# Expert layers of a routed language-model block: per-expert results summed in PSUM instead of stored and reloaded, and both layers of a group taken in a row

## The reference, cut to what matters

```python
# b = 32 sequences, s = 128 tokens, d = 256; E = 32 experts, K = 8, hidden width 1024
probs = jax.nn.softmax(x @ gate_w.T + gate_b, axis=-2)
vals, idx = top_k(probs, K, over the tokens)           # per sequence and expert
merged = jnp.einsum('bked,bke->bed', tok, vals)        # tok: the picked rows of x
h = gelu(jnp.einsum('bei,eih->beh', concat(merged, 1), w1))   # w1: 32 x 257 x 1024
o = jnp.einsum('bej,ejo->beo', concat(h, 1), w2)              # w2: 32 x 1025 x 256
out_tok = jnp.einsum('beo,bke->bkeo', o, vals)
out = zeros.at[b, idx].add(out_tok)                    # each pick's weighted result to its token
return h2 + out
```

## Time and profile before

| | us |
|---|---|
| median of 3 runs | 860.63 (858.05 to 862.29) |
| profiled execution, whole | 859.29 |
| its span, first to last instruction | 857.5 |
| PE, DVE, ACT, POOL busy in the span | 704.5, 608.4, 348.6, 447.3 |

### The profile page before, as it was taken

The page is one execution under the profiler, slowest core; times in us unless marked ns, Lnnn a source line. Parts: engine busy times, 40 slices in busy tenths (PEclk is TensorE's granted clock), DMA queues, the critical chain, the costliest instruction groups (busy, mean ns, idle before and its releaser), DMA issues. The chain is left out here.

```text
span 857.5 us, 20594 instructions
## 1 busy us (share of the span) xinstructions
PE 704.5 (82%) x7892; PEld 484.9 (57%) x7892; DVE 608.4 (71%) x863; ACT 348.6 (41%) x553; POOL 447.3 (52%) x250
## 2 busy tenths in 40 slices
PE   6577679878999999999999999994899859866755
PEld 4356544437777777777777777763677624322333
DVE  3688558889999999999999999992477631001124
ACT  3366534443544545544554444542455431100000
POOL 1788300004999999999999999992121100000000
PEclk9699989997999999999999999996999969999998
DMA  4100000000001010000000000002953159999985
GB/s 113 50 2 0 0 0 0 0 1 15 14 14 34 14 37 12 12 6 12 12 12 11 8 12 12 15 15 61 412 180 121 49 225 387 415 420 417 416 274 196
DMA packets 47295, 85.89 MB, mean 100 GB/s; under 512 B 5552, under 2 KB 30192, under 8 KB 47120
## 3 DMA queue, kind: packets, MB, share of 16 engines
q1 hardware_dynamic: 41920, 81.07, 25.8%
q10 hardware_dynamic: 5328, 4.17, 1.6%
HBM read 76.04 MB, written 9.18 MB: 99 GB/s over the span
## 5 line engine op out<-in xcount | busy, mean ns | idle before, releaser
L909 POOL TENSOR_TENSOR read<-state,q_pos 128x1024 f32<-128x1024 f32 x128 | 300.3, 2365 | 28.7 <-DVE state L1018 22.5
L1018 DVE TENSOR_TENSOR_SCAN state<-fac,ps_up 128x1024 f32<-128x1024 f32 x128 | 290.0, 2277 | 8.6 <-ACT fac L953 8.2
L953 ACT ACTIVATE fac<-ps_xf 128x1016 f32<-128x1016 f32 x128 | 130.3, 1018 | 175.7 <-PE ps_xf L1052 162.4
L1052 PEld LDWEIGHTS ps_xf<-hot,xtab 64*128 64x128 f32 x2048 | 126.6, 190 | 58.0 <-ACT fac L953 43.8
L1052 PE MATMUL ps_xf<-hot,xtab 64*128 64x128 f32 x2048 | 149.5, 286 | 10.9 <-ACT fac L953 8.8
L1052 PE MATMUL ps_up<-hot,utab 64*128 64x128 f32 x2048 | 140.8, 277 | 17.5 <-DVE state L1018 17.5
L1052 PEld LDWEIGHTS ps_up<-hot,utab 64*128 64x128 f32 x2048 | 127.2, 190 | 23.0 <-issue 16.4
L918 POOL TENSOR_TENSOR utab<-tab 128x1024 f32 (+1 forms) x32 | 64.5, 2016 | 94.6 <-SPq L86 94.6
L1097 PE MATMUL ps_o<-read,misc 128*32 128x256 f32 x1024 | 82.1, 392 | 4.1 <-POOL read L909 4.1
L1008 DVE TENSOR_TENSOR xtab<-tab,ps_k 128x1024 f32<-128x1024 f32 x64 | 59.5, 929 | 2.0 <-PE ps_k L1044 2.0
L1692 DVE COPY h_t<-ps_e 128x512 f32<-128x512 f32 x16 | 10.3, 686 | 59.6 <-PE ps_e L1756 59.6
(11 more groups left out here) (233 smaller groups left out, 973.7 us busy)
## 6 DMA issues: line engine op xcount, KB each, us to landing
early<-in_L_ffn_w SPq DMA_DIRECT2D x19, 2048.0 KB, 17.7
pair_tab<-in_L_ffn_w SPq DMA_DIRECT2D x5, 2048.0 KB, 23.4
late<-in_L_ffn_w SPq DMA_DIRECT2D x3, 2048.0 KB, 23.5
zy<-in_L_ffn_w SPq DMA_DIRECT2D x3, 1536.0 KB, 21.8
rec_out<-osb SPq DMA_DIRECT2D x128, 32.0 KB, 1.5
late<-rec_out SPq DMA_DIRECT2D x8, 512.0 KB, 4.1
pair_tab<-in_L_ffn_w SPq DMA_DIRECT2D x4, 512.0 KB, 3.5
early<-in_L_ffn_w SPq DMA_DIRECT2D x2, 1024.0 KB, 24.6
```

What stands on the lines that cost most here:

```text
L909: nc.gpsimd.tensor_tensor(read[n % 2][:], state[n % 4][:].rearrange("p (b i t) -> p b i t", b=2, i=IB), q_pos[x.s][:, :, x.k].unsqueeze(2) ...
L953: nc.scalar.activation(fac[n % 2][:].rearrange("p (n t) -> p n t", t=T)[:, :, 1:], ps_x[:].rearrange("p (n t) -> p n t", t=T)[:, :, 1:], A ...
L1018: nc.vector.tensor_tensor_scan(state[n % 4][:], fac[n % 2][:], ps_u[n % 2][:], 0.0, ALU.mult, ALU.add)\
L1052: last = nc.tensor.matmul(dst[:, b * 512 + col * T:b * 512 + (col + 1) * T], stationary[rows], pos[rows], start=True, stop=True)
```

## The change

All eight groups take the same way. The order of the blocks is first layer and second layer of group 0, then of group 1, and so on. `ps_1` is there once, in the PSUM banks in which the transposes also land; the four banks that it leaves hold `ps_s`, the results in their final arrangement, over the whole part. After the first layer of group g, PE runs `spread_rows(g-1)`: eight products of a zero-one matrix, cut out of a wide tile `spread` at a shifted column, with `eo`, which add the group g-1 into all rows of `ps_s`. So `exp_out`, its six stores, its four reloading transfers, the zeroing of `oq` and the sum on DVE are gone; DVE copies `ps_s` to `oq` once (L1684 of the changed kernel). Group 7 keeps its own way. `eo` is there once. The biases of both layers lie in one tile `bias`, and `sel` therefore is written on 64 partitions by two copies in place of one. The last block is one transfer like all others. The helpers `strip` and the reordered zero-one matrix `by_row` are made in the freed slot after group 5.

```diff
@@ def expert_halves():
-    order = [(1, g, h) for g in range(2) for h in range(2)]
-    for g in range(X // QB):
-        order += [(2, g, h) for h in range(2)]
-        if g + 2 < X // QB:
-            order += [(1, g + 2, h) for h in range(2)]
-    return order
+    return [(layer, g, h) for g in range(X // QB) for layer in (1, 2) for h in range(2)]
@@ def experts(nc, a, m, sem, sb, out):
-    eo = sb("eo", [P, 2, E])
+    eo = sb("eo", [P, E])
+    spread = sb("spread", [P, QUADS * P + X])
...
-        ps_1 = [ps[:, 2 * s:2 * s + 2].rearrange("p n c -> p (n c)") for s in range(2)]
+        ps_s = ps[:, 0:4].rearrange("p n (q e) -> p (n q) e", e=E)
+        ps_1 = ps[:, 4:6].rearrange("p n c -> p (n c)")
         ps_t = ps[:, 4:6].rearrange("p n (h q) -> p (n h) q", q=P)
@@ scalar
-            def store(g):
-                act.wait_ge(eo_ok, START + g + 1)
-                act.dma_start(exp_out[QB * g:QB * (g + 1)].rearrange("x b e -> (x b) e"),
-                              eo[:, g % 2]).then_inc(eo_st[g % 2], 16)
-
             for g in range(GROUPS):
                 hidden(g)
-                if 0 < g < GROUPS - 1:
-                    store(g - 1)
                 if g + 2 < GROUPS:
                     selections(g + 2)
-            act.wait_ge(row_ok, ZEROS)
-            src = exp_out.rearrange("x (q j) e -> j x q e", j=QB)
-            for j in range(QB):
-                act.dma_start(oq[j * X:j * X + STORED], src[j, 0:STORED]).then_inc(f_ld, 16)
@@ sync
-                if n < len(wt.order) - 1:
-                    wt.load_all(sp, n)
-                else:
-                    wt.transfer(sp, n, 0, QB, slice(0, HID // 2)).then_inc(wt_head, 16)
-                    wt.load(sp, n, 0, QB, slice(HID // 2, HID))
+                wt.load_all(sp, n)
@@ vector
             for g in range(GROUPS):
...
                 if g == GROUPS - 1:
-                    dve.wait_ge(row_mm, SPREAD_MM)
-                    dve.wait_ge(f_ld, START + 16 * QB)
-                    nc.vector.tensor_tensor(oq, oq, ps_s, ALU.add).then_inc(row_ok, 1)
+                    dve.wait_ge(sp_mm, START + GROUPS - 1)
+                    nc.vector.tensor_copy(oq, ps_s).then_inc(row_ok, 1)
                 results(g)
+                if g == GROUPS - 3:
+                    ch.link(nc.vector.memset(strip, 0.0))
+                    nc.vector.tensor_copy(by_row, ident[:].rearrange("p (n j) -> p j n", j=QB))
+                    nc.vector.tensor_copy(strip.rearrange("p (x q) -> p q x", q=QUADS)[:, QUADS - 1, 0:QB],
+                                          at_row[:, X - QB:X]).then_inc(row_ok, 1)
+                    dve.wait_ge(pick_mm, START + 1)
+                    nc.vector.tensor_copy(last_picks, ps_t).then_inc(row_ok, 1)
@@ tensor
             def first_layer(g):
-                s = g % 2
-                pe.wait_ge(gl, START + g - 1)
+                if g > 0:
+                    pe.wait_ge(htok, START + 2 * g)
...
+            def spread_rows(g):
+
+                pe.wait_ge(row_ok, SPREAD)
+                pe.wait_ge(eo_ok, START + g + 1)
+                for q in range(QUADS):
+                    at = q * P + X - QB * (g + 1)
+                    last = nc.tensor.matmul(ps_s[:, q], spread[:, at:at + P], eo[:], start=g == 0 and q % 2 == 0, stop=g == GROUPS - 2,
+                                            skip_group_check=True)
+                last.then_inc(sp_mm, 1)
...
-            first_layer(0)
-            first_layer(1)
-            for g in range(GROUPS - 1):
+            for g in range(GROUPS):
+                first_layer(g)
+                if g > 0:
+                    spread_rows(g - 1)
                 transpose_hidden(g)
-                second_bias(g)
-                for h in range(2):
-                    second_layer(g, h)
+                second_layer(g)
                 if g == GROUPS - 3:
                     picks_of_last()
-                if g + 2 < GROUPS:
-                    first_layer(g + 2)
-                if g == GROUPS - 3:
-                    pe.wait_ge(row_ok, PICKS)
-
-            transpose_hidden(GROUPS - 1)
-            second_bias(GROUPS - 1)
-            spread_rows()
-            second_layer(GROUPS - 1, 0)
+
             pe.wait_ge(row_ok, SUMS)
             output_stored(0)
-            second_layer(GROUPS - 1, 1)
             rows_of_last()
```

More of the change, by code:

```diff
@@ L32 @@
 HT = HID // P
-STORED = X - 2 * QB
 EPS = 1e-5
@@ L1582, in experts @@
 def experts(nc, a, m, sem, sb, out):
-    ident, merged, exp_out, h2, picked = m["ident"], m["merged"], m["exp_out"], m["h2"], m["picked"]
-    wt, stored = m["wt"], m["stored"]
-    b1, b2 = sb("b1_sb", [X, HID]), sb("b2_sb", [X, E])
-    sel = [sb(f"sel{s}", [X, QB, B]) for s in range(2)]
+    ident, merged, h2, picked = m["ident"], m["merged"], m["h2"], m["picked"]
+    wt, late = m["wt"], m["stored"]
+    bias = sb("bias", [2 * X, HID])
+    b1, b2 = bias[0:X], bias[X:2 * X, 0:E]
+    sel = [sb(f"sel{s}", [2 * X, QB, B]) for s in range(2)]
     hg = sb("hg", [P, HID])
     h_t = sb("h_t", [P, HT, P])
-    eo = sb("eo", [P, 2, E])
-    oq = stored[:, 0:QUADS * E].rearrange("p (q e) -> p q e", e=E)
-    last_picks = stored[:, QUADS * E:QUADS * (E + T)].rearrange("p (q t) -> p q t", t=T)
-    last_rows = stored[:, QUADS * (E + T):QUADS * (E + T) + E]
-    strip = sb("strip", [P, QUADS + X])
+    eo = sb("eo", [P, E])
     at_row, at_expert = sb("at_row", [P, B]), sb("at_expert", [P, X])
-    spread = merged[:, 0]
+    spread = sb("spread", [P, QUADS * P + X])
+    oq = late[:, 0:QUADS * E].rearrange("p (q e) -> p q e", e=E)
+    last_picks = late[:, QUADS * E:QUADS * (E + T)].rearrange("p (q t) -> p q t", t=T)
+    last_rows, by_row, strip = (late[:, lo:lo + n] for lo, n in ((3072, E), (3328, P), (3456, QUADS + X)))
     GROUPS = X // QB
@@ L1631, in selections @@
                     after(act, 2, g - 2, 1)
-                nc.scalar.copy(sel[g % 2][:], ident[0:X, QB * g:QB * (g + 1)].unsqueeze(2)
-                               .broadcast_to([X, QB, B])).then_inc(sel_ok, 1)
+                for lo in (0, X):
+                    last = nc.scalar.copy(sel[g % 2][lo:lo + X], ident[lo:lo + X, lo + QB * g:lo + QB * (g + 1)]
+                                          .unsqueeze(2).broadcast_to([X, QB, B]))
+                last.then_inc(sel_ok, 1)
             def hidden(g):
@@ L1757, in transpose_hidden, with second_layer @@
                     last.then_inc(ht, 1)
-            def second_bias(g):
-                pe.wait_ge(eo_ok, START + g - 1)
-                nc.tensor.matmul(ps_2[g % 2][:, 0:E], sel[g % 2][:].rearrange("x j b -> x (j b)"), b2[:],
+            def second_layer(g):
+                if g > 1:
+                    pe.wait_ge(eo_ok, START + g - 1)
+                nc.tensor.matmul(ps_2[:, g % 2], sel[g % 2][X:2 * X].rearrange("x j b -> x (j b)"), b2,
                                  start=True, stop=False, skip_group_check=True)
-            def second_layer(g, h):
-                s = g % 2
-                n_half = wt.at[2, g, h]
-                if n_half == len(wt.order) - 1:
-                    pe.wait_ge(wt_head, START + 16)
-                else:
-                    wt.wait(pe, n_half)
-                pe.wait_ge(htok, START + 2 * g + h + 1)
-                for n in range(h * HT // 2, (h + 1) * HT // 2):
-                    if n_half == len(wt.order) - 1 and n == HT - HT // 4:
+                for n in range(HT):
+                    h, at = divmod(n, HT // 2)
+                    n_half = wt.at[2, g, h]
+                    if at == 0:
@@ L1774, in second_layer @@
                         wt.wait(pe, n_half)
+                        pe.wait_ge(htok, START + 2 * g + h + 1)
                     for j in range(QB):
-                        last = nc.tensor.matmul(ps_2[s][j * B:(j + 1) * B, 0:E], h_t[:, n, j * B:(j + 1) * B],
-                                                wt.block(n_half, j, slice(n % (HT // 2) * E, (n % (HT // 2) + 1) * E)),
+                        last = nc.tensor.matmul(ps_2[j * B:(j + 1) * B, g % 2], h_t[:, n, j * B:(j + 1) * B],
+                                                wt.block(n_half, j, slice(at * E, (at + 1) * E)),
@@ L1789, in picks_of_last @@
                                                 start=True, stop=True)
-                last.then_inc(row_mm, 1)
-            def spread_rows():
-                pe.wait_ge(row_ok, SPREAD)
-                pe.wait_ge(gl, START + GROUPS)
-                for q in range(QUADS):
-                    last = nc.tensor.matmul(ps_s[:, q], spread[:, QB * q:QB * (q + 1)].rearrange("p j x -> p (j x)"),
-                                            eo[:, 0], start=True, stop=True)
-                last.then_inc(row_mm, 1)
+                last.then_inc(pick_mm, 1)
+                pe.wait_ge(row_ok, PICKS)
             def rows_of_last():
```

71 lines of the change are left out of this document (29 added, 42 removed).

## The result

| | before | changed |
|---|---|---|
| median, us | 859.34 (857.78 to 862.29, 4 runs) | 848.42 (845.83 to 850.42, 4 runs) |
| profiled execution, whole | 859.29 | 850.42 |
| its span | 857.5 | 848.7 |
| PE's first product of the experts' part | 703.20 | 701.42 |
| copy of the last `eo` | 839.81 | 830.64 |

The ratio of the changed kernel to the one before is 0.9869, with a 95% interval of 0.9843 to 0.9894: 1.3% faster, clear of the noise, and the median lies 1.2 us from the 849.6 that was forecast.

The account below looks back on a forecast made before the run. Weight transfers set the pace, then the reload of `exp_out` held the end; moving the last `eo` copy from 839.81 to 829.3, less 0.2, gives -10.3 us: span 847.2, time 849.6 us, range 846.0 to 854.0.

Parts of the forecast that it names:

- The forecast's chain behind b29: After group 7's second first-layer block: first layer, bias, `spread_rows`, transposes, second layer in series, 12.9 us, ending at 829.3.
- b29 usable, rel: Group 7's second first-layer block was to be usable 113.25 us after PE's first product of the experts' part.
- b29's products and bias: Second half of group 7's first layer, 1.83 us, and the bias after it, 1.91: forecast 3.74.
- `spread_rows` to the copy of the last `eo`: Group 7's end: `spread_rows` 3.72 us, then transposes through second layer to the copy of `eo`; forecast 9.15.
- The stores: Six 128 KB stores ahead of b29 in the weight stream; dropping them makes b29 usable 1.9 us earlier.
- "Does the stream stay full?": Start of the stream: b11 needs b2 used, which was forecast in time with some 2 us remaining; cost 0.
- the second rival: The stream gains nothing: stores cost no time, or b11 comes 2 us late; 851.5 us, chance 0.08.
- PE per group: PE's work in each group, `spread_rows` included: 14.36 us, hidden within the 20.2 us that four blocks take.
- The rival of PE as the bound: PE mildly the bound over the groups: each costs 1.6 us more than its rows; 852.5 us, chance 0.15.
- The clock: PE at b29: a 3.1 us wait ahead, like earlier 2.4 GHz cases, so 1.83 us; lower clock adds 1.6.
- b29 at the lower clock: Rival: b29's products in group 7 run at the lower clock, 1.6 us more; 851.2 us, chance 0.17.
- `ps_s`: DVE's copy of `ps_s` at the end was to finish about 0.8 us before PE asks for it; cost 0.

Follow-up runs that it names:

- e2: Kernel before without the four reloading transfers, six stores kept (results of groups 0 to 5 left out of the output): 848.79 us, ratio 0.9866.
- e3: Kernel before without the reload and without the six stores: 850.48 us, ratio 0.9890.
- e4: Changed kernel with the six stores of 128 KB put back on ACT's queue, read by nothing: 850.41 us, ratio 0.9877 to the kernel before.
- e7: Changed kernel with the old order for groups 0 and 1, both first layers ahead of both second layers: 849.17 us, ratio 0.9880 to the kernel before.
- e5: Changed kernel with group 6's spreading products moved between b28 and b29, in PE's wait: 848.45 us, ratio 0.9867 to the kernel before.
- e6: Changed kernel with six useless spreading-shape products in PE's wait between b28 and b29: 848.93 us, ratio 0.9890 to the kernel before.
- e8: Changed kernel with four more spreading-shape products behind the spreading of groups 0 to 5: 852.17 us, ratio 0.9910 to the kernel before.
- e10: Changed kernel with old order for groups 0 and 1, last spreading between b28 and b29, last block in two halves: 848.91 us, ratio 0.9883 to the kernel before.
- e12: Changed kernel with old order for groups 0 and 1 and last spreading between b28 and b29, last block whole: 848.83 us, ratio 0.9889 to the kernel before.
- e11: Changed kernel with old order for groups 0 and 1, last spreading ahead of b28, last block in two halves: 850.28 us, ratio 0.9882 to the kernel before.

## Why the prediction was right, and where it was not

**The mechanism held.** The chain before ran over the reload, and without it (e2 alone) the time falls by as much as with the whole change. What the sums in PSUM and the new order are worth apart from each other is not shown: no run has the one without the other. The forecast's chain behind b29 is the measured one, link by link.

**The sum was 3.3 us too short.** It put the part at 154.3 - 10.3 = 144.0; it took 147.3. On the common zero, by the forecast's own steps:

| step | forecast | measured | difference |
|---|---|---|---|
| b29 usable, rel | 113.25 | 114.92 | +1.67 |
| b29's products and bias | 3.74 | 5.42 | +1.68 |
| `spread_rows` to the copy of the last `eo` | 9.15 | 8.88 | -0.27 |
| from there to the end | 17.9 | 18.06 | +0.16 |

- *The stores*, 1.9 us: right as far as two pairs of profiles tell, 1.97 in e3 and 1.93 in e4.
- *"Does the stream stay full?", cost taken 0*: mis-sized, 1.7 us in the three profiles of the changed kernel. The step that failed is b2's time. Group 0's second layer was counted from rows at 2.4 GHz, so that b2 was done 11.4 us after the first product with 2 us to spare. It stands behind Gelu's 1.11 us, uncovered in the first group, and ran partly at 1.2 GHz:

```profile
709.47 1.16 PE L1729 MATMUL ps_e<-ident,hg 128*128 128x128 f32 x8 [1.11 <-ACT hg L1633]
710.57 0.73 PE L1735 MATMUL ps_e<-bias,sel 32*128 32x256 f32 x2
711.22 5.26 PE L1744 MATMUL ps_e<-early,h_t 128*32 128x256 f32 x64
```

  5.26 instead of about 3.6. b11's issue came at 13.41, 2.0 us after the forecast's 11.4, which is all of the reserve. By the forecast's own figures this would still have cost nothing, so the reserve was counted too large as well; e7, with b11 at 8.84, still shows 378 GB/s from 715 to 720. In the changed kernel's two windows behind b11's issue, (420 - 320) x 5 = 0.5 MB and (420 - 397) x 5 = 0.1 MB are missing, 1.5 us of the stream by an estimate from those rows. This was half of the second rival, which had given b11 2 us, and e7 supports it: with the old front b29 came 1.7 us earlier than in the changed kernel (b28 0.5 to 0.8 us earlier than in e5 and e6).
- *PE per group*: 14.36 forecast. Measured 14.1 (first products of group 2 at 730.40, of group 3 at 744.49), and group 6 began to wait for b25 as forecast. PE waited 1.58 us for b21 in group 5 too, which the forecast did not count; it did not reach the end. The rival of PE as the bound was too dark; with 10.3 us more work (e8) PE only just became it.
- *The clock*: the forecast took 1.83 for b29's products since the wait ahead, 3.1 us by its sum, was like the 3.08 and 3.13 of the earlier trace rows and not like 3.23. The wait was 2.95, shorter still, and the products took 3.14, the bias 2.42. The rival "b29 at the lower clock", 1.6 us, is what happened, and it was worth 1.66 (5.42 us from b29's first product to the end of its bias, and 3.76 in e6). The error was the criterion: the length of the wait does not decide. After 2.35 (changed kernel) and 2.33 (e7) the same b28 took 1.92 and 3.42.
- *`ps_s`*: forecast to be ready 0.8 us before PE asks. Measured 1.1:

```profile
827.16 2.28 DVE L1684 COPY pair_tab<-ps_e 128x2048 f32<-128x2048 f32 x1
830.64 0.42 DVE L1677 COPY eo<-ps_e 128x256 f32<-128x256 f32 x1 [1.20 <-PE ps_e L1744]
```

**Why the median fitted.** That is luck in good part. The part was 3.3 us longer than forecast, the profiled execution began it 1.8 us earlier, and the median of the four runs lies 2.0 below the profiled one, where the forecast had it 0.6 above. The absolute times that the forecast named fit better than they deserve too: b29 at 816.34 for 816.45, b28 at 811.47 for 811.4. The repeats, 852.7 twice, are the fairer number, and they too lie in the range of 846.0 to 854.0.

The Trainium skill, "TensorE: Matmul & The Clock Gate", section "HAM oscillation", tells of a kernel whose PE works for about 2 us and then waits about 3 to 5 us for a transfer, over and over, and whose every burst starts at half clock. b29 agrees in the three profiles of the changed kernel (3.14, 3.14 and 3.07 us behind waits of 2.95, 2.95 and 2.94), and so does b28 in e4 (3.55 behind 3.09). The kernel before does not agree in two of its waits, 3.08 and 3.13 us with 1.92 behind each. b28's other waits, 2.33 to 2.53 us, are shorter than those of the page, and the runs have both clocks behind them: 1.92 in the changed kernel, its repeats and e5, and 3.36 to 3.42 in e6, e7, e10 and e12.

## What to carry to other kernels

Ask of a bundle of edits which one of them takes the last link off the chain: here the reload alone was worth all of the gain, and the saved stores, though real, were spent elsewhere. Work that PE owes anyway can go into its last waits, ahead of the products that stand in series at the end: this was worth 2 us in e5, and nothing in e10 and e12, where the clock was low elsewhere, so it has to be measured each time. Useless work in the same wait is not shown to help. When the order of a ring of buffers is changed, work out the first few releases with the durations that hold at that place, and not with those of the steady state: 2 us of reserve at b11 were gone in one second layer at the lower clock.

## What was not expected of the hardware

- A gap of 1.11 us behind continuous work was followed by a stretch at 1.2 GHz: the second layer of group 0 took 5.16 to 5.31 in the seven profiles that have the new order from the start, and the last one 5.35, 6.19 and 5.35 in e10, e11 and e12. In e5 the same gap of 1.11 was followed by 1.93 and 1.93. No rule for which of these it will be came out of the runs; that stays open.
- b28's and b29's products were never both slow in the new order. Where b28's ran at 1.2 GHz (e4, e6, e7, e10, e12), b29's ran at 2.4 GHz, behind waits, filler or spreading alike; the changed kernel and its repeats had it the other way round. So a run that changes what stands ahead of b29 has to be read together with b28.
- The stream moved 413 to 423 GB/s in the windows 750 to 755 and 780 to 785 of all fourteen profiles, stores or none, and once it has run thin it does not catch up: b29 was 1.7 us late, 100 us after the weak stretch.
